# One-hots two halves ahead, score products first, and a turned node stage in a graph kernel on one core

## The reference

```
# L0, for each of 8 heads, and again for one head over the 512 concatenated values
msg = feat @ W
scores = leaky_relu((msg @ a[:dh])[src] + (msg @ a[dh:])[dst], 0.2)
e = exp(scores - scores.max())
out = segment_sum(msg[src] * (e / segment_sum(e, dst)[dst])[:, None], dst)
out = (out - mean) * rsqrt(var + 1e-5) * gamma + beta     # statistics over the nodes
# after the second one
x = layernorm(x + out + x @ W_res + b_res)                 # the node stage of this change
# L1, twice: mean of x[src] over the edges of dst, @ Wl.T, + x @ Wr.T + b, fixed norm (relu between)
# then layernorm(x + that)
```

## Time and profile before

| | us |
|---|---|
| median of three runs | 9471.22 (9467.75 to 9473.85) |
| the profiled execution | 9472.38 |
| its span | 9470.8 |

### The profile page before, as it was taken

The page is one execution under the profiler, slowest core; times in us unless marked ns, Lnnn a source line. Parts: engine busy times, 40 slices in busy tenths (PEclk is TensorE's granted clock), DMA queues, the critical chain, the costliest instruction groups (busy, mean ns, idle before and its releaser), DMA issues.

```text
span 9470.8 us, 196466 instructions
## 1 busy us (share of the span) xinstructions
PE 5802.7 (61%) x50950; PEld 4110.0 (43%) x50951; DVE 4811.3 (51%) x14633; ACT 3083.3 (33%) x7540; POOL 5048.4 (53%) x4726
## 2 busy tenths in 40 slices
PE   3355565555556454555555555547588877488887
PEld 2344444444444224555455555535344444244444
DVE  5344444444444645555555555555555555355555
ACT  0111111010111113444444444441255555355555
POOL 1454555546464015555555555512466666466676
PEclk9756665665666575555555555555699998799999
DMA  3222121222212442222222222202344444344444
GB/s 92 43 44 59 44 58 46 45 59 45 59 44 57 137 110 42 41 41 41 41 41 41 41 41 41 41 15 73 79 111 112 110 110 108 92 107 109 108 108 101
DMA packets 622304, 647.34 MB, mean 68 GB/s; under 512 B 343902, under 2 KB 515637, under 8 KB 621872
## 3 DMA queue, kind: packets, MB, share of 16 engines
q0 software_dynamic: 193600, 384.69, 19.3%
q1 hardware_dynamic: 356987, 238.04, 8.8%
q10 hardware_dynamic: 71640, 23.81, 1.0%
HBM read 562.39 MB, written 83.23 MB: 68 GB/s over the span
## 4 chain that ended last, share of the span: by engine, by line
issue 21%; DVE 21%; another core or an unknown queue 19%; PE 18%; DVEq 9%; DMA 5%; ACT 4%; SPq 1%; ACTq 1%; POOL 0%; POOLq 0%
PE psa L1412 7%; PE psc L1429 5%; ACT acc L1161 2%; DVE acc L1825 2%; DMA acc<-y_d 2%; DVEq L1786 1%; DVEq L593 1%; DVE den L1822 1%; DMA t_gat<-acc 1%; DVE rows L1894 1%; PE psc L1400 1%; DVEq L1790 1%; DMA t_part<-den 1%; DVE acc L1685 1%
## 5 line engine op out<-in xcount | busy, mean ns | idle before, releaser
L613 POOL DMA_INDIRECT rows<-t_gat,idx x3168 | 3081.7, 973 | 2408.9 <-issue 824.2
L633 POOL DMA_INDIRECT acc<-t_part,acc x1400 | 1795.9, 1283 | 822.1 <-issue 618.8
L1338 PE MATMUL psa<-rhs,rows 128*128 128x176 f32 (+1 forms) x6336 | 1721.4, 431 | 55.5 <-issue 33.4
L1161 ACT ACTIVATE acc<-psa 128x384 bf16<-128x384 f32 x3200 | 1345.8, 503 | 1226.2 <-PE psa L1412 656.3
L1338 PEld LDWEIGHTS psa<-rhs,rows 128*128 128x128 f32 x6336 | 1503.9, 312 | 162.8 <-issue 98.1
L1412 PE MATMUL psa<-den,rhs 125*32 125x384 bf16 x12800 | 909.0, 361 | 452.8 <-ACT acc L1161 313.4
L1326 PE MATMUL psc<-oh,wgt 128*8 128x22 f32 (+1 forms) x6336 | 294.6, 207 | 1036.3 <-ACT wgt L1067 872.1
L1061 ACT ACTIVATE oht<-psc 22x1024 bf16<-22x1024 bf16 x402 | 407.3, 1013 | 1594.1 <-remote 1110.9
L1412 PEld LDWEIGHTS psa<-den,rhs 125*32 125x32 bf16 x12800 | 296.0, 98 | 1056.1 <-ACT acc L1161 633.3
L1326 PEld LDWEIGHTS psc<-oh,wgt 128*8 128x8 f32 (+1 forms) x6336 | 238.1, 95 | 1146.4 <-ACT wgt L1067 960.6
L1067 ACT ACTIVATE wgt<-s_d 128x64 f32<-128x64 f32 (+1 forms) x396 | 93.8, 237 | 1965.4 <-DVE s_d L1742 1249.9
(11 more groups left out here) (342 smaller groups left out, 8216.4 us busy)
## 6 DMA issues: line engine op xcount, KB each, us to landing
rows<-list_src SPq DMA_DIRECT2D x200, 500.0 KB
rows<-t_gat,idx POOLq DMA_INDIRECT x3168
acc<-y_d SPq DMA_DIRECT2D x50, 1000.0 KB, 5.4
y_d<-stg SPq DMA_DIRECT2D x100, 250.0 KB, 2.0
acc<-t_part,acc POOLq DMA_INDIRECT x1400
acc<-t_sage SPq DMA_DIRECT2D x300, 62.5 KB
adw<-win_d SPq DMA_DIRECT2D x820, 2.2 KB
adw<-win_d SPq DMA_DIRECT2D x788, 0.4 KB
```

The lines of the kernel that those rows point to most:

```text
L613: eng.indirect_dma_start(rows[:, j, 0:spec["width"]], None, spec["table"], bass.IndirectOffsetOnAxis(ap=idx[:, j:j + 1], axis=0)).then_inc ...
L633: eng.indirect_dma_start(h_prow[u][:, t, :], None, t_parts[layer], bass.IndirectOffsetOnAxis(ap=h_idx[u][:, t:t + 1], axis=0)).then_inc(h_ ...
L1161: eng.activation(h_rows[:, g, :], psa[:, g % 4, 0:D3], ACT.Copy).then_inc(hyb["ev"], 1)
L1338: last = eng.matmul(sums(half, q, h), rows[:, slot * TH + j, 0:D], right, start=(j == 2 * q), stop=(j == 2 * q + 1))
```

## The change

One-hots are made two halves ahead in the two weighted passes (`lead` 2 on DVE, ACT and PE; SP keeps 1), so `oh` has one buffer for each ring slot. On PE the score products of the next half stand at the head of `main`, behind a wait for `exp_arg`. On ACT the list copies (`evict`, `counted`) come ahead of the front. DVE does `entries` ahead of `index_list`, SP its list load behind the windows. The node stage is turned: the product with W_res is made as columns (W_res by xT, 500 columns at once), b_res is added to the batch norm's shift once, DVE adds aT and that product into `mT`, PE turns the sum back, and DVE adds x from there. Rounds of two chunks overlap: the residual of two, then centre and scale of the two before. Rows and parts get four buffers instead of two.

```diff
+def by_lagged_pairs(eng, in_table, round_):
+    def four(e, lead, first_old, second_old):
+        round_(e, (0, 1), (-2, -1) if lead else (), first_old)
+        round_(e, (2, 3), (0, 1), second_old)
...
-        oh = sb("oh", [EP, 2, TH, WIN])
+        oh = sb("oh", [EP, RING, TH, WIN])
...
-        zt = part(acc, NP_, 12544 + 8 * TC * D, 2, TC, D)
+        zt = part(acc, NP_, 12544 + 4 * TC * D, 4, TC, D)
...
-        def halves(eng, spec, lo, hi, nxt, front, main):
+        def halves(eng, spec, lead, lo, hi, nxt, front, main):
             slots = spec["slots"]
-            front(lo, 0, True)
+            for slot in range(lead):
+                front(lo, slot, slot == 0)
             with eng.Fori(lo, hi, spec["step"]) as b:
-                for slot in range(slots - 1):
-                    main(b, slot, lambda: front(b, slot + 1, False))
+                for slot in range(slots - lead):
+                    main(b, slot, lambda: front(b, slot + lead, False))
                 ahead = next_trip(eng, spec, nxt, b)
-                main(b, slots - 1, lambda: front(ahead, 0, False))
+                for slot in range(slots - lead, slots):
+                    main(b, slot, lambda: front(ahead, slot + lead - slots, False))
...
# SP, main
-                    if lists and slot % 2 == 0:
-                        list_load(block_of(spec, b, slot))
                     next_front()
+                    if lists and slot % 2 == 0:
+                        list_load(block_of(spec, b, slot))
...
# ACT, main of a pass
                 eng.activation(wgt[:, half, :, 0:h], s_d[:, :, 0:h], ACT.Exp).then_inc(wgt_ready, 1)
+                if lists and half == 0:
+                    evict(blk)
+                if lists and half == 1:
+                    counted(value(eng, lists[0], MAX_BLOCKS))
                 next_front()
                 if lists and half == 0:
-                    evict(blk)
                     squares(True)
                 if lists and half == 1:
-                    counted(value(eng, lists[0], MAX_BLOCKS))
                     store_idx(blk)
                     squares(False)
...
# PE, a pass
             def scores(half):
-                f = value(eng, nf)
-                eng.wait_ge(oht_sb, f)
+                eng.wait_ge(oht_sb, value(eng, nf) + 1)
...
                 if spec["weighted"]:
+                    eng.wait_ge(exp_arg, m)
+                    eng.sem_inc(alone, 1)
+                    scores(1 - half)
                     eng.wait_ge(wgt_ready, m)
...
                 next_front()
                 for q in range(PAIRS):
-                    if q == PAIRS // 2 and spec["weighted"]:
-                        scores(1 - half)
...
# PE, node stage
             def products(e, u):
-                eng.wait_ge(S["msb"], e + (u + 3))
-                eng.wait_ge(S["acp"], e + (u + 1))
                 eng.wait_ge(S["xsb"], e + (u + 3))
+                eng.wait_ge(S["zt"], e + (NC + u + 1))
+                eng.matmul(psa[0:D, u % 2, 0:CH], weights, xT[:, u % 2, :], start=True, stop=True).then_inc(S["mps"], 1)
+
+            def turn_back(e, u):
+                eng.wait_ge(S["zt"], e + (NC + u + 3))
+                eng.wait_ge(S["msb"], e + (u + 3))
                 for t in range(TC):
-                    o = psa[0:NP_, u % 2, t * D:(t + 1) * D]
-                    cols = slice(t * NP_, (t + 1) * NP_)
-                    eng.matmul(o, aT[:, u % 2, cols], left_w, start=True, stop=False)
-                    eng.matmul(o, xT[:, u % 2, cols], right_w, start=False, stop=False)
-                    last = eng.matmul(o, ones[0:1, 0:NP_], bias, start=False, stop=True)
-                last.then_inc(S["mps"], 1)
+                    last = eng.transpose(psa[0:NP_, 2 + u % 2, t * D:(t + 1) * D], mT[u % 2][:, t * NP_:(t + 1) * NP_], ident[:, :])
+                last.then_inc(S["tps"], 1)
...
# DVE, a pass
-                        eng.wait_ge(adx_ready, value(eng, nf) + 2)
+                        eng.wait_ge(adx_ready, eng.snap(nk, min_val=0, max_val=MAX_HALVES) + 3)
...
-                        index_list()
                         entries()
+                        index_list()
...
# DVE, node stage
             batch_norm(1, go[:, :], bo[:, :], 2)
+            link(tt(shf[:, 0:1], shf[:, 0:1], bres[:, :], ALU.add))
...
+                def residual(e, u):
+                    eng.wait_ge(S["mps"], e + (u + 3))
+                    eng.wait_ge(S["acp"], e + (u + 1))
+                    eng.wait_ge(S["tps"], e + (NC + u + 1))
+                    eng.sem_inc(alone, 1)
+                    tt(mT[u % 2], aT[:, u % 2, :], psa[0:D, u % 2, 0:CH], ALU.add).then_inc(S["zt"], 1)
...
-                by_four_from_table(eng, KB // (4 * TC), lambda e, u, table: centre(e, u), scale)
+                def round_(e, now, old, table):
+                    for u in now:
+                        residual(e, u)
+                    for u in old:
+                        centre(e, u)
+                    for u in old:
+                        scale(e, u, table)
+                by_lagged_pairs(eng, KB // (4 * TC), round_)
```

More of the change, by code:

```diff
@@ L718, in _ @@
                     eng.sem_inc(s_, 2)
+            eng.sem_inc(n_fin["stored"], 2)
             eng.sem_inc(lst["out"], 48)
@@ L818, in run @@
                 first_of_next(v, lo, w0)
-                halves(eng, spec, lo, hi, nxt[0], front, main)
+                halves(eng, spec, 1, lo, hi, nxt[0], front, main)
             def after(s):
@@ L1058, in front @@
                     eng.wait_ge(oh_ready, f)
-                    eng.activation(ohb[:, half, :, :], oh[:, half, :, :], ACT.Copy).then_inc(ohb_ready, 1)
+                    eng.activation(ohb[:, half, :, :], oh[:, slot, :, :], ACT.Copy).then_inc(ohb_ready, 1)
                 eng.wait_ge(oht_ps, f)
@@ L1082, in after @@
                     eng.activation(stg[:, u, :], psa[:, u, 0:CH], ACT.Copy).then_inc(fl_sb, 1)
-            node_ranges(eng, spec, lambda s0, v, lo, hi, w0: halves(eng, spec, lo, hi, nxt, front, main), after)
+            node_ranges(eng, spec, lambda s0, v, lo, hi, w0: halves(eng, spec, spec["lead"], lo, hi, nxt, front, main), after)
             if lists:
@@ L1135, in deviation @@
                 eng.activation(lnr[:, u % 2, :], lnr[:, u % 2, :], ACT.Sqrt).then_inc(S["std"], 1)
-            def pair(stages, e, chunks):
-                for stage in stages:
-                    for u in chunks:
-                        stage(e, u)
-            pair([copies], 0, (0, 1))
-            with eng.Fori(0, NC // 2 - 1) as i:
-                pair([copies], i * 2, (2, 3))
-                pair([deviation], i * 2, (0, 1))
-            pair([copies], NC - 1, range(NC % 2))
-            pair([deviation], NC // 2 * 2 - 2, (0, 1))
-            pair([deviation], NC - 1, range(NC % 2))
+            def round_(e, now, old, table):
+                for u in now:
+                    copies(e, u)
+                for u in old:
+                    deviation(e, u)
+            by_lagged_pairs(eng, KB // (4 * TC), round_)
         def act_step(eng, layer):
@@ L1294, in front @@
                     return
+                if first:
+                    eng.wait_ge(oht_sb, value(eng, nf))
+                    eng.sem_inc(alone, 1)
                 eng.wait_ge(ohb_ready, value(eng, nf))
@@ L1326, in main @@
                         last = eng.matmul(p_dens[half][0:hd, (j // 2) * WIN:(j // 2 + 1) * WIN], wgt[:, half, j, 0:hd],
-                                          oh[:, half, j, :], start=(j % 2 == 0), stop=(j % 2 == 1))
+                                          oh[:, slot, j, :], start=(j % 2 == 0), stop=(j % 2 == 1))
                     last.then_inc(den_ps, 1)
@@ L1336, in main @@
                     for j in (2 * q, 2 * q + 1):
-                        right = rhs[:, half, j, 0:h * WIN] if spec["weighted"] else oh[:, half, j, :]
+                        right = rhs[:, half, j, 0:h * WIN] if spec["weighted"] else oh[:, slot, j, :]
                         last = eng.matmul(sums(half, q, h), rows[:, slot * TH + j, 0:D], right,
@@ L1367, in run @@
                     eng.matmul(sums(1, q, h), zeros[:, :], ones[:, 0:h * WIN], start=True, stop=True).then_inc(sums_ps, 1)
-                halves(eng, spec, lo, hi, nxt, front, main)
+                halves(eng, spec, spec["lead"], lo, hi, nxt, front, main)
             node_ranges(eng, spec, run, after)
@@ L1765, in weighted_onehot_half @@
                         eng.wait_ge(wgt_ready, m)
-                        eng.tensor_tensor(rhs[:, half, :, 0:WIN], oh[:, half, :, :], wgt[:, half, :, 0:1].to_broadcast([EP, TH, WIN]),
+                        eng.tensor_tensor(rhs[:, half, :, 0:WIN], oh[:, slot, :, :], wgt[:, half, :, 0:1].to_broadcast([EP, TH, WIN]),
                                           ALU.mult).then_inc(rhs_ready, PAIRS)
```

85 lines of the change are left out of this document (54 added, 31 removed).

## The result

| | before | changed |
|---|---|---|
| median | 9472.5 us | 9825.0 us (9813.6 to 9840.8, 4 runs) |
| ratio | | 1.037 (95% interval 1.036 to 1.039) |
| profiled execution | 9472.4 us | 9840.8 us |
| first pass, first to last gather | 2731.9 us | 2836.6 us (+104.7) |
| second pass, the same | 2657.0 us | 2986.6 us (+329.6) |

The account below looks back on a forecast made before the run. No engine was near full; stops of POOL's gathers, with PE's semaphores seen late, were taken to bound the passes. 9472.4 - 130 (first pass) + 0 (second pass) - 80 (node stage) = 9262 us, range 9080 to 9460.

Parts of the forecast that it names:

- The reading of the stops: Both passes: PE's semaphores given during back-to-back gathers are seen 1.1 us after groups of four, 1.8 after eight.
- rival E: Both passes: no stops are left, 10.0 us a half, whole kernel 8110 us; chance 0.04.
- First pass: -130 forecast: First pass: one stop a half releases four pairs, two halves 24.4 us against 25.75, so -130 us.
- 7.4 us of work ... under the 9.7 us in which POOL issues eight gathers: First pass: PE does a half without an intermediate wait in 7.4 us, within eight gathers' 9.7 us.
- Second pass: 0 forecast: Second pass: list work offsets the gain, 26 to 29 us a block around today's 27.07, 0 us.
- 29.0 as the bound: Second pass: slow bound of the block's time, 29.0 us, +190 us.
- Rival C: Second pass: one more stop, pairs released singly while POOL idles, 30 us a block, +287, 9549 us; chance 0.10.
- C's own sign, small groups: Second pass, list half: gathers in groups of two, two and four, 3.8 + 3.8 + 6.6 in place of 6.6 + 6.6.
- Node stage: -80 forecast: Node stage: DVE becomes the bound at 8.0 us a chunk against 12.1, some 20 us given back, -80 us.
- The rest at nothing: Outside the main terms: one more one-hot group before each pass and the bias added to the shift once, 0 us.
- Rival D: Passes: the stop is PE's own work, untouched; only the node stage gains, 9392 us; chance 0.07.

Follow-up runs that it names:

- the third group: Runs on another chip, against the kernel before at 8053.8 us: the changed kernel, 7897.0 us, and the kernel before with only the turned node stage, 7976.8 us.
- the rest: Changed kernel, with POOL waiting after the fourth gather of every half until these four have landed: 9236.2 us, ratio 0.9761.
- the middle order: Changed kernel with PE's scores and transposes put back behind the second pair of sums: 9401.1 us, ratio 0.9939; later, on another chip, 8090.2 us, ratio 1.0054.
- node stage alone: Kernel before with only the turned node stage, both passes as before: 9378.1 us, ratio 0.9915; later, on another chip, 7976.8 us, ratio 0.9902.

## Why the prediction was wrong, point by point

*The reading of the stops held in the main.* That PE's semaphores are late while POOL issues back to back, and that copy, DVE and POOL start in one bunch behind a group, is what the rows of after show again. It was too simple in two places. Of 1147 semaphores of PE in the first pass of the kernel before whose product ends within a group, 347 come before the group's end, mostly of products that end in its first 3 us; the late ones do come 1.1 us (median) after groups of four and 1.7 after groups of eight. And DVE's semaphores are late too. Where the stops are absent the changed kernel takes 7897 us and the kernel before 8050. For the changed kernel with no stop left I had worked out 8110 (rival E) and given it 0.04, as a limit and not as a thing that a chip does.

*First pass: -130 forecast, +105 measured.* The groups of eight and the one stop a half came. The step that failed is "7.4 us of work ... under the 9.7 us in which POOL issues eight gathers". It took PE's durations from groups of four and of eight in which PE issues 32 and 40 products (medians of the first pass of before; up to 42 and 46 in nineteen of twenty), and used them in one that should hold all 64 of a half (24, 16, 8, 16). Past about 45 each further product takes 0.7 to 1.4 us. From the first score product to the last sum product a half takes 13.6 us (median) in the changed kernel where 7.4 were forecast, and the same 64 take 6.4 us in the third group, where nothing crawls. Scores at the head push transposes and sums past that point, and the sums are what POOL waits for: two halves in 27.0 us (median) against 24.4 forecast. Where less of what POOL waits for stands behind the crawl (the rest, the middle order) the same pass gives 24.9 and 25.0, that is the 24.4 to 0.5 us.

*Second pass: 0 forecast, +330 measured.* The term that failed is the block's time, taken at today's 27.07 us with 29.0 as the bound; the median is 30.5. Rival C has the size (30 us) but not the mechanism: the groups did not fall apart into two and two, they grew to eight and eight (176 groups of eight, where the kernel before had one), and with them came the crawl of PE (706 late products against 37) and more of DVE's gaps. C's own sign, small groups, isn't in the trace. C also kept the first pass's gain, so its 9549 was still 276 us short. The part of ACT's order is there and measured, but it is some 50 us.

*Node stage: -80 forecast, -69 measured* between the passes, -81 in the median of the kernel with that part alone, and -77 without stops. The period is 9.03 us, not 8.0: DVE is busy 169.1 of 216.7 us (7.05 a chunk), and 21.2 us of the rest it waits for the 500-column product (L1516), which takes two records of 0.86 us. The forecast had it nearly without gaps.

*The rest at nothing:* +2.8 us, right.

*Rival D* (the stop is PE's own work; 9392 us) is refuted: the same products on the other chips give their semaphores at once, PE crawls only in groups of gathers and up to 2 us behind them, and a kernel with an added wait for POOL that becomes 589 us faster can't be bound by PE's work. Whether a product ends late or only its semaphore is seen late, which D also asked, the modelled ends don't tell.

*Small slips in the working:* POOL is busy 55.6% of the first pass, not 57%, and eight gathers with a stop of 2.6 us make 12.26, so two halves 24.5 us. Neither changes the forecast.

What stays open: why one chip delays semaphores and lets engines crawl while POOL issues gathers, and others don't, and whether it is the chip at all or something else that ran on it then; whether issuing or transfers do it; whether the recording of every instruction for the trace has a part in it (no run here tests it; the profiled execution of before, 9472.4 us, is no longer than the others, 9467.8 to 9476.6); what is counted by the 45 products (in the second pass, whose products are smaller in part, the onset lies at 49 to 64). The groups that should tell fell on chips without the effect. The effect of the rest and of the orders is shown; the mechanism behind the crawl is not.

## What to carry to other kernels

A duration holds for the surroundings in which it was read: before adding work to a stretch, look whether the stretch is one in which the engine is let through only so far, and put what others wait for first in its queue and what nobody waits for last. A stop of a busy issuer isn't lost time by itself: here 2.5 us of ordered rest at the right place saved 589 us on one chip, and cost 647 on another (there with the old order; neither kernel was run with the rest on both). And a comparison of two kernels on one chip is a statement on that chip: the order of before, changed and middle came out as 2, 3, 1 on the one and 2, 1, 3 on the others.

## What the runs showed of the hardware

- Unchanged kernel, same inputs: 9459 to 9472 us on one chip, 8048 to 8066 us in groups on four others, each group within 0.4% in itself. The granted clock doesn't explain it: in the second pass it is 0.50 on both sides.
- In a free first pass POOL issues 320 gathers in a row at 1.245 us each or a little more (16 in 20.4 us), and PE's semaphores arrive 0.01 us after the shown end. On the first chip two thirds of those whose product ends within a group (first pass, kernel before) arrive after the group's end, 1.1 us after groups of four and 1.7 after groups of eight (medians). DVE's are late as well (35% by over 0.5 us against 1%, node stage alone).
- On the first chip, about 45 products after a group's first gather, PE goes on in steps of 0.7 and 1.4 us; DVE's small operations show gaps of 1.3 us beside it (second pass).
- The gathers of the two mean layers show it as well: 716 gathers take 1331 us in groups of seven with 1.9 us between (first of the two, node stage alone, first chip) and 1188 us in groups of 112 on the third group's.
- The gathers' packets of 4352 bytes take 292 ns on the first chip and 262 on the third group's (medians, first pass, node stage alone); SP's of 2000 bytes take 82 ns on both.
